# A graph layer on one Trainium2 core: four moves in the order of work around its attention loop

## What is computed

```python
xn = layernorm(x)
# 1. graph term: softmax over 4 heads for the edges of each token, heads summed
x  = x + gnn(xn, src, dst)
#         + mix(xn): a linear attention between hyperbolic maps
h   = relu(batchnorm(conv(logmap(xn))))          # 768 channels: q, k, v
s   = pointwise(depthwise(h)); t2 = scaled(concat(h, s))
q, k, v = split(t2); out = (v * sum(relu(k))) * relu(q) / (sum(v) + eps)
ft  = res(scaled(out)) + b_res                   # called u in the kernel
x  = x + gnn + expmap(ft)                        # expmap: tanh(norm) * u / norm
# 2. mixture of two of eight experts, one routing decision for all tokens
x  = x + layernorm(experts(layernorm(x)) + ...)
```

## Time and profile before

| | us |
|---|---|
| median of 3 runs | 827.18 (826.77 to 827.38) |
| the profiled execution | 826.45 |
| its span in the trace | 824.6 |
| PE busy | 780.2 (95%) |
| DVE, ACT, POOL busy | 519.0, 425.2, 383.2 |
| mean granted clock of PE | 0.986 |
| the attention loop: first to last `turn_norms` (24 steps) | 215.25 to 448.94 |
| the tail to the routing decision | 449 to 471 |

### The profile page before, as it was taken

How to read it: one execution, slowest core, us unless ns; L and a number is a source line. 1 busy time by engine, 2 the same in 40 slices (tenths; PEclk the granted TensorE clock), 3 DMA queues, 4 the chain that set the end, 5 groups by cost and what they waited for, 6 DMA issues and landing times. The chain is left out here.

```text
span 824.6 us, 15099 instructions
## 1 busy us (share of the span) xinstructions
PE 780.2 (95%) x5056; PEld 639.4 (78%) x5056; DVE 519.0 (63%) x1475; ACT 425.2 (52%) x969; POOL 383.2 (46%) x601
## 2 busy tenths in 40 slices
PE   5899999999889999999489899999999999999996
PEld 5678888888566666667356788888888888888885
DVE  6863488797678988887989625353535343434345
ACT  2566436888779998888466242222223232323230
POOL 2430878877358788888447403131313121212222
PEclk9999999999999999999889999999999999999999
DMA  8855122222012121111100040000000000000000
GB/s 215 208 153 149 42 58 55 55 52 51 14 51 60 38 65 27 56 52 47 42 24 24 19 122 14 25 15 23 16 22 17 22 17 21 19 20 20 18 22 29
DMA packets 35420, 41.31 MB, mean 50 GB/s; under 512 B 11520, under 2 KB 20696, under 8 KB 35339
## 3 DMA queue, kind: packets, MB, share of 16 engines
q1 hardware_dynamic: 22355, 30.71, 13.0%
q0 software_dynamic: 8000, 6.82, 3.8%
q10 hardware_dynamic: 4984, 2.79, 1.5%
HBM read 25.59 MB, written 14.60 MB: 49 GB/s over the span
## 5 line engine op out<-in xcount | busy, mean ns | idle before, releaser
L951 ACT ACTIVATE Z<-ps,b1s 128x250 f32<-128x250 f32 x200 | 93.5, 469 | 233.1 <-PE ps L1231 233.1
L1244 PE MATMUL ps<-Z 128*125 128x256 f32 x800 | 176.5, 379 | 0.0
L1231 PE MATMUL ps<-Z 128*128 128x250 f32 x800 | 173.3, 374 | 0.0
L1244 PEld LDWEIGHTS ps<-Z 128*125 128x125 f32 x800 | 150.1, 188 | 22.3
L1231 PEld LDWEIGHTS ps<-Z 128*128 128x128 f32 x800 | 151.3, 189 | 17.9
L1025 PE MATMUL ps<-Z,L 128*128 128x250 f32 x600 | 126.9, 373 | 0.0
L663 POOL TENSOR_SCALAR zr<-zmv 125x1 f32<-125x1 f32 x50 | 11.1, 221 | 248.7 <-issue 240.1
L1025 PEld LDWEIGHTS ps<-Z,L 128*128 128x128 f32 x600 | 113.6, 189 | 13.2
L1826 DVE TENSOR_TENSOR Z<-ps,L 125x256 f32<-125x256 f32 x50 | 21.2, 425 | 160.6 <-PE ps L1244 160.6
L1145 PE MATMUL ps<-wr,Z 128*125 128x256 f32 x400 | 92.6, 384 | 0.0
L790 ACT ACTIVATE Z<-Z,bn_o,bn_s 128x250 f32<-128x250 f32 x150 | 81.3, 598 | 1.0 <-DVE bn_o L1535 1.0
(11 more groups left out here) (221 smaller groups left out, 1273.8 us busy)
## 6 DMA issues: line engine op xcount, KB each, us to landing
Z<-in_x SPq DMA_DIRECT2D x25, 250.0 KB
out<-Z SPq DMA_DIRECT2D x24, 250.0 KB
xt_table<-L SPq DMA_DIRECT2D x25, 231.0 KB
Z<-in_x SPq DMA_DIRECT2D x1, 2016.0 KB
g_table<-gt SPq DMA_DIRECT2D x25, 62.5 KB
gr<-g_table SPq DMA_DIRECT2D x25, 62.5 KB
Z<-in_x SPq DMA_DIRECT2D x1, 1344.0 KB
Z<-in_w SPq DMA_DIRECT2D x2, 512.0 KB, 3.4
```

Of the source, the lines that this page charges most:

```text
L951: a_.activation(ge[:, b % 2, f, :], ps[:, f % 4, 0:BT], ACT.Gelu, bias=b1s[:, f // NF, f % NF:f % NF + 1]).then_inc(gelu_done.sem, 1)
L1231: last = mm(ps[:, f % 4, 0:BT], w1s[:, f // NF, k, (f % NF) * 128:(f % NF + 1) * 128], h_of(b, k), start=(k == 0), stop=(k == KD - 1))
L1244: last = mm(ps[0:TP, 4 + 2 * (b % 2) + t, 0:D], ge[:, b % 2, f, t * TP:(t + 1) * TP], w2s[:, f // NF, f % NF, :], start=(f == 0), stop=(f ...
```

## The change

Four moves of existing calls; no instruction is added or removed.

1. POOL, step 2: `add_edge(0)` is called behind `scale_of_u(0)` instead of ahead of it (block 1 already was; blocks 2 on stay ahead).
2. ACT, before the loop: the last pair's `edge_softmax` stands ahead of `square_s(0, R_K)`, `keep_k(0)` and `square_s(0, R_Q)`.
3. ACT, loop: the five late relus of Q are made in steps 1, 1, 2, 3, 4 instead of 3, 4, 5, 6, 7, at the same place within a step.
4. Tail: ACT's `square_o(24)` stands ahead of `keep_xn(21)`, and PE's `norms(25)` ahead of `res_half(24, 0)`.

```diff
-        EARLY_RELU, EARLY_Q, RELU_AT = 30, 20, 3
+        EARLY_RELU, EARLY_Q, RELU_AT = 30, 20, (1, 1, 2, 3, 4)
...
-                (2, lambda b: add_edge(b) if b != 1 else None),
+                (2, lambda b: add_edge(b) if b >= 2 else None),
                 (3, rstd_of_x1),
                 (2, scale_of_u),
                 (2, lambda b: gather_piece(b) if b >= 2 else None),
-                (2, lambda b: add_edge(b) if b == 1 else None),
+                (2, lambda b: add_edge(b) if b < 2 else None),
...
             def more_relu(s):
 
-                b = EARLY_Q + s - RELU_AT
-                if EARLY_Q <= b < NB:
-                    relu(b, R_Q, relu_q)
+                for i, at_step in enumerate(RELU_AT):
+                    if s == at_step:
+                        relu(EARLY_Q + i, R_Q, relu_q)
...
+            edge_softmax(EARLY // 2 - 1)
             square_s(0, R_K)
             keep_k(0)
             square_s(0, R_Q)
-            edge_softmax(EARLY // 2 - 1)
             act.wait_ge(bn_done.sem, bn_done.count(2))
             relu(0, R_V, relu_v)
...
             tanh(NB - 3)
+            square_o(NB - 1)
             keep_xn(NB - 4)
-            square_o(NB - 1)
             square_u(NB - 2)
...
             turn_xn(NB - 4)
+            norms(NB)
             res_half(NB - 1, 0)
-            norms(NB)
             turn_norms(NB)
             res_half(NB - 1, 1)
```

## The result

The changed kernel takes 823.6 us, the median of 8 runs (820.96 to 825.55). The kernel before, on the same chip, has a median of 825.31 us over 8 runs (824.12 to 827.38); the three runs that stood ahead of the prediction were the highest of these. These two medians differ by 1.7 us. The ratio on record, which is not the quotient of the medians, is 0.9966 with a 95% interval of 0.9952 to 0.9979: 0.34% or 2.8 us faster, between 1.7 and 4.0. So the size of the gain is known to a microsecond or so. The profiled execution took 822.4 us against 826.45, with a span of 820.6 us against 824.6 and a mean granted clock of 0.984 against 0.986.

A forecast was written before the change was run, and what follows sets the result against it. PE was taken as busy 95% of the span, so time lay in its gaps or longer chains on other engines. 0.35 + 1.5 + 1.13 + 0.93 = 3.9 us gave a median of 823.3 us, range 821.9 to 825.9.

The forecast's parts named there:

- Border: Before the loop: the earlier exponential removes DVE's wait and brings ACT's L828 forward; gain 0.35 us, bounds 0.1 and 0.35.
- Scale ahead of edge term: Steps 2 and 3: POOL's scale runs in its idle time, so tanh and L1671 come sooner; gain 1.5 us, between 1.28 and 1.8.
- PE's 1.28: Step 3: PE's wait in front of `pointwise_v(3)`, which can come at most 1.28 us sooner.
- a load takes 4.6 us (228.89 to 233.51): Block 1's load, issued when `res(1)` ends, lands near 242.3; POOL arrives at 242.1 and waits 0.2 us.
- the 243 that it had named as a sign of being wrong: A load of block 1 landing after 243 us would make the prediction wrong.
- The moved L619: POOL's third scale instruction, now beside DVE's L1576, may take 0.3 us more, covered by 1.2 us until ACT is free.
- Relus: Blocks 4 to 7: without late relus ACT is not full; gain 1.13 us, bounds -0.3 to 1.13, steps 1 and 2 unharmed.
- The next step, without a late relu, takes 8.93: Step behind block 7: 8.93 us, used against the rival that DVE or POOL would be late.
- rival (a): Loop: part of the gain is absorbed by DVE, POOL or PE; gain 2.4 us, time 824.8 us, chance 0.20.
- Tail: Tail: `square_o(24)` leaves the chain behind `keep_xn(21)`, so the routing's relay comes earlier; gain 0.93 us, bounds 0.5 and 0.93.
- Rival (c): Step 1: less idle time ahead keeps PE at 2.4 GHz; together 0.4 us more gain, 822.9 us, chance 0.10.
- the 2.30 gap would shrink by as much: Step 1: at full clock ACT's 2.30 us wait for PE shrinks by up to 0.9, so two relus stick out by 0.5.

The follow-up runs named there:

- e_exp: Kernel before with only the last pair's exponential moved ahead of the squares before the loop; 825.39 us, ratio 0.9986.
- e_relu: Kernel before with only the five late relus of Q moved to steps 1, 1, 2, 3, 4; 826.24 us, ratio 1.001.
- v_over: Changed kernel with the late relus in steps 1, 1, 2, 2, 2, so three blocks in step 2; 825.56 us in one run.
- b_again: Kernel before, run again with no edit on another chip; 825.61 us.
- a_again: Changed kernel, run again with no edit; 824.46 us, ratio 0.9971 to the kernel before.
- v_land: Changed kernel with the edge term's load ahead of x, and block 2's x held until block 1's has landed; 825.3 us, ratio 0.9974.
- e_scale: Kernel before with only the edge term moved behind u's scale in step 2; 826.28 us, ratio 1.0002.
- v_gr: Changed kernel with SP issuing a block's edge-term load ahead of its x; 823.63 us, ratio 0.9951 to the kernel before.

## Why the prediction came out

*Border.* 0.35 us was expected; 0.30 (`e_exp`) to 0.42 (changed kernel) was found. The chain was read rightly, DVE's wait being the one that counted.

*Scale ahead of edge term.* Step 2-3 fell by 1.67 to 1.93 against the two traces of the kernel before; expected were 1.3 to 1.8. PE's 1.28 was not its limit: `norms(3)` came sooner as well, as the prediction said. The mis-sized term is the one behind it, "a load takes 4.6 us (228.89 to 233.51)", which was block 0's time, taken over for block 1. By the same ruler, from SP's L477 to POOL's start, block 1 takes 5.33 us (236.72 to 242.05), and from L475, the load of x, 5.64 against 4.93 (233.51 - 228.58). Either way it is 0.7 longer, and why is open. So POOL waits 0.86 instead of 0.2, and step 3-4 grows by 0.52 to 0.56. The net is 1.1 to 1.4, not 1.5. Counted from the issue at 237.7 that the prediction took, the landing would be at 243.1, just past the 243 that it had named as a sign of being wrong; in the changed kernel's own time it is 242.05. The early start of L1671 was over-sized too: against `turn_norms(2)` it comes 1.6 us earlier (2.47 behind it instead of 4.05), not 1.8.

*The moved L619.* Expected was up to 0.3 more in its new place, beside DVE's L1576. In the changed kernel DVE reaches L1576 at 231.03 and is at its end (0.68) when L619 starts at 231.59, which took 0.19: the two meet for 0.12 us and it took no longer than its 0.19 elsewhere. The 0.49 of the earlier trace rows is found again in later steps, as in `e_relu` at 270.27 and 279.47.

*Relus.* 1.13 was expected in 4 to 7, and 0.95 to 1.12 came. The step that failed is "The next step, without a late relu, takes 8.93", from which the prediction took PE as the next bound: that step takes 8.93 when the steps before it are slow by ACT. Once they are not, the chain through DVE and POOL is late, and 0.35 comes back in 7 to 9. This is rival (a), which foresaw DVE or POOL late instead of ACT: it put the relus' part at 0.3, and 0.6 to 0.8 is left of 1.13. The relus in steps 1 and 2 cost nothing, as foreseen, and `v_over` shows that two blocks more would not have fitted.

*Tail.* 0.93 was expected; 0.91 is in the relay from `keep_xn(21)` to `scale_of_u(23)`, and 0.92 in the whole tail (16.23 against 17.15).

*The clock.* Rival (c) held the half clock for something that the change could take away, and "the 2.30 gap would shrink by as much" for its consequence. Both fail: the dip comes and goes by itself in the same kernel, and in `b_again` at full clock the gap is 2.06, not 1.4. The row:

```profile
223.17 0.38 ACT L886 ACTIVATE L<-ps 128x250 f32<-128x250 f32 x1 [2.06 <-PE ps L1126]
```

*The sum.* Border 0.4, scale 1.1 to 1.4, relus 0.6 to 0.8 and tail 0.9 make 3.0 to 3.5 us by the stages. From `turn_norms(0)` to the first L1201 it is 249.23 us in `b_again`, 246.48 in the changed kernel and 247.17 in `a_again`; with the border's 0.4 that is 3.2 and 2.5 us less, and 0.5 of the 0.7 between these two is in one step that the change doesn't touch (block 20 to 21: 24.60, 24.68 and 25.19). The ratios say 2.8 and 2.4. The prediction's 3.9 was too much by 0.4 to 0.9 by the stages and by 1.1 by the ratio; 0.1 to 0.4 of it is block 1's load and about 0.4 the relus, and what is left is within the spread. By the ratio the gain lies nearer to rival (a)'s 2.4 than to the forecast. The time of 823.3 us is near the 823.6 by luck: the gain was taken off 827.2 us, the median of three runs, and eight runs gave 825.3, 1.9 less. By the medians the change gained 1.7 us, 2.2 less than the 3.9. The two errors went opposite ways and left 0.3. What was right is the direction, the waits that the four moves take away, and the sizes of border and tail; what was too high is the gain in the loop.

## What to carry to other kernels

A wait that an order of calls makes can be read off the timeline and priced to a tenth of a microsecond; what is easily missed is what the freed engine meets next. The time of one load was not the time of the next of its kind (4.6 and 5.3 us by the same ruler), so give such a term a range. A step that runs at the bound's pace beside slow neighbours does not prove that the other engines can keep that pace when all steps do. When the parts are smaller than the spread of the runs, compare stage by stage in traces, with an unchanged copy of the kernel among them, before anything is put down to the change.

## What the runs showed of the chip

- The granted clock in step 1 is not a property of the program: with the same PE instructions it was 0.57 in 218 to 222 us in two of 12 traces (step 0-1 of 9.15 and 9.20 us) and 1.00 in ten (8.04 to 8.14). Without the fillers, with PE idle for 2.68 us, it was 0.50 in the one trace taken. At the border it was 0.50 from 209 to 214 us in one trace of 14 (`v_land`), with a border of 11.94 us instead of 8.93 to 9.86.
- Block 1's load of x, 250 KB, took 4.90 to 6.41 us from issue to the start of its reader in step 4 (`v_land` 4.90, `e_scale` 5.36, `a_again` 5.60, changed kernel 5.64, `v_gr` 5.84, `v_over` 6.41; the reader's bracket names a DMA in each, and where the edge term's small load is issued behind x it can be that one). Block 0's took 4.24 to 5.66 in the same traces, always less than block 1's. Why is open.
- What lies ahead of the loop is a large part of the spread from trace to trace: `turn_norms(0)` starts at 214.64 to 219.89 us, though no edit touches what lies before 205 us. That is wider than the whole change. The step at block 20, which takes the long division, was 24.57 to 25.91 us, which is about half of it.
